# A two-layer Perceiver block on one core: a second cross attention queued by pairs of key tiles, three context buffers in the first, and GpSimd waits at three normalisations

## The reference

```python
x = x + _L0_xattn_ref(_layernorm(x, axis=-1), ctx_1024, L0_xattn_Wq, ...)       # one head of 128
x = x + _L0_attn_ref(_layernorm(x, axis=-1), ...)                               # 16 heads of 8
x = x + _L0_ffn_ref(_layernorm(x, axis=-1), L0_ffn_gate, ...)                   # experts, top 2
x = x + _L1_xattn_ref(_layernorm(x, axis=-1), ctx_1024, mask_Bx1x1xS2_ff0, ...) # 16 heads of 8
x = x + _L1_attn_ref(_layernorm(x, axis=-1), ...)                               # fake-quantised
x = x + _L1_ffn_ref(_layernorm(x, axis=-1), ...)                                # experts, top 2
```

```python
k = _split_heads(ctx @ kw + kb)
v = _split_heads(ctx @ vw + vb)
scores = jnp.einsum('bqhd,bkhd->bhqk', q, k) / np.sqrt(D // H).astype(np.float32)
scores = scores + mask
probs = jax.nn.softmax(scores, axis=-1)
out = jnp.einsum('bhqk,bkhd->bqhd', probs, v)
```

## Time and profile before

| | us |
|---|---|
| median of 3 runs | 1500.36 (1500.07 to 1515.0) |
| profiled execution | 1504.1 |
| its span | 1502.3 |
| start and first normalisation | 0 to 32.3 |
| first cross attention | 32.3 to 182.0 |
| a0 and the first experts | 182.0 to 528 |
| second cross attention, its first slots | 528 to 565 |
| its slots with scores and maxima | 565.0 to 1079.9 |
| the rest | to 1502.3 |

### The profile page before, as it was taken

The page is one execution under the profiler, slowest core; times in us unless marked ns, Lnnn a source line. Parts: engine busy times, 40 slices in busy tenths (PEclk is TensorE's granted clock), DMA queues, the critical chain, the costliest instruction groups (busy, mean ns, idle before and its releaser), DMA issues.

```text
span 1502.3 us, 24995 instructions
## 1 busy us (share of the span) xinstructions
PE 1132.7 (75%) x9454; PEld 829.9 (55%) x9454; DVE 784.9 (52%) x1546; ACT 495.5 (33%) x656; POOL 228.9 (15%) x234
## 2 busy tenths in 40 slices
PE   3766667588888358889989898898957644756987
PEld 2545444467777136666666666666644532545776
DVE  4223358543334355566666666556447547855111
ACT  0322223112222114544554454554513210321332
POOL 2000024202220200111111111111015101411110
PEclk9778869679999568999999999999979677766999
DMA  7444300101120133444434333343100000010111
GB/s 183 164 160 161 131 1 1 42 1 42 42 82 3 42 89 91 108 110 107 102 90 110 89 89 89 89 107 85 35 1 1 1 0 1 1 28 1 43 28 28
DMA packets 44859, 96.78 MB, mean 64 GB/s; under 512 B 12600, under 2 KB 28624, under 8 KB 44800
## 3 DMA queue, kind: packets, MB, share of 16 engines
q1 hardware_dynamic: 44800, 95.96, 24.2%
HBM read 41.04 MB, written 13.84 MB: 37 GB/s over the span
## 4 chain that ended last, share of the span: by engine, by line
PE 50%; issue 16%; DVE 14%; DMA 7%; POOL 5%; SPq 4%; ACT 3%; DVEq 0%; POOLq 0%; ACTq 0%
PE PS L261 46%; DMA KS<-kl 4%; DVE mx L1568 3%; PE PS L1192 2%; DVE u_all L274 2%; DVE kl L1557 2%; POOL work_area L389 2%; SPq L904 1%; DMA expert_area<-in_ctx 1%; DMA early<-in_ctx 1%; SPq L896 1%; POOL PT L389 1%; PE PS L1208 1%; PE PS L291 1%; POOL rstd_all L280 1%
## 5 line engine op out<-in xcount | busy, mean ns | idle before, releaser
L1568 DVE TENSOR_REDUCE mx<-PS 128x1 f32<-128x512 f32 (+1 forms) x512 | 278.3, 570 | 103.4 <-PE PS L261 96.0
L1135 ACT ACTIVATE PT<-PS 128x1024 f32<-128x1024 f32 (+1 forms) x208 | 212.3, 1021 | 62.6 <-PE PS L261 62.6
L261 PE MATMUL PS<-KS,QB 128*128 128x512 f32 (+1 forms) x512 | 178.9, 419 | 42.7 <-DVE mx L1568 22.1
L261 PE MATMUL PS<-QB,KS 128*128 128x256 f32 (+1 forms) x832 | 165.4, 321 | 18.6 <-DMA QB<-nml 18.6
L261 PE MATMUL PS<-QB,QS 128*128 128x512 f32 x576 | 158.0, 422 | 23.8 <-DVE wcol L662 21.7
L261 PEld LDWEIGHTS PS<-QB,KS 128*128 128x128 f32 (+1 forms) x832 | 115.7, 187 | 52.3 <-issue 28.1
L261 PEld LDWEIGHTS PS<-KS,QB 128*128 128x128 f32 x512 | 90.0, 191 | 94.9 <-issue 48.4
L261 PEld LDWEIGHTS PS<-QB,QS 128*128 128x128 f32 x576 | 108.7, 200 | 60.6 <-issue 26.8
L674 DVE SCALAR_TENSOR_TENSOR x<-PS,wcol,x 128x128 f32<-128x128 f32 x128 | 44.9, 351 | 137.0 <-PE PS L261 133.6
L291 PE MATMUL PS<-consts,u_all 128*128 128x128 f32 x64 | 15.7, 426 | 104.2 <-DVE u_all L274 83.6
L1121 ACT ACTIVATE kh<-PS,c_L_xattn_ck_b 128x512 fp32r<-128x512 f32 x64 | 38.1, 595 | 147.8 <-PE PS L261 123.7
(11 more groups left out here) (246 smaller groups left out, 1726.1 us busy)
## 6 DMA issues: line engine op xcount, KB each, us to landing
KS<-kh SPq DMA_DIRECT2D x128, 200.1 KB, 4.1
context_transposed<-ctxT SPq DMA_DIRECT2D x16, 800.5 KB, 3.5
ctxT<-context_transposed SPq DMA_DIRECT2D x16, 800.5 KB, 4.3
KS<-kl SPq DMA_DIRECT2D x64, 200.1 KB, 4.0
early<-in_ctx SPq DMA_DIRECT2D x8, 768.0 KB
expert_area<-in_ctx SPq DMA_DIRECT2D x8, 768.0 KB
expert_area<-in_L_ffn_experts_w SPq DMA_DIRECT2D x24, 256.0 KB, 3.2
expert_area<-in_L_ffn_W SPq DMA_DIRECT2D x16, 256.0 KB, 3.0
```

Of the source, the lines that this page charges most:

```text
L261: return T.matmul(o, l, r, start=start, stop=stop, **k)
L1135: P["exp_a"].done(S.activation(PT[0:rows, par, :], PS[0:rows, 1024 + 1024 * par:2048 + 1024 * par], ACT.Exp), f"e{k}")
L1568: P["max_v"].done(V.reduce_max(mx[:, p, c:c + 1], bank((4 * p + c) % 2, CHUNKS[c][1]), AX), item)
```

## The change

There are four parts.

1. First cross attention: a third context buffer in the free end of `work_area`. Pair n uses buffer n % 3; the load of pair 2 is issued behind the weights at the start, and later ones one pair earlier than before. The loops are written out, and TensorE takes the queries straight from `l0qk_all`, which moves to `u_all`.
2. GpSimd waits, at three of the nine normalisations, until VectorE has done its eight instructions.
3. In the attentions the row group alternates from matmul to matmul, instead of the bank or the block.
4. Second cross attention: tiles are grouped by two (`GROUPS`), with a second place for probabilities (`PT_TILES`), and the values of both tiles stand in one block of 16 matmuls. `steps(n)` reads one table for all engines. Key projections stand amid the maxima of a group, v2 and v3 at the end of the slot, and VectorE takes `sum` and each `kl` at the very place that they have in the table. SyncE issues the load of context n+2 between the first and the second key stack of slot n.

The diff, cut to its core:

```diff
-        ctx_nat = [a[:, :].rearrange("p (b k d) -> p b k d", b=2, k=KT) for a in (early, expert_area)]
         work_area = sb("work_area", [128, 3584 + KT * 256])
         tail_area, value_area = work_area[:, 0:3584], work_area[:, 3584:3584 + KT * 256]
+        ctx_nat = [a.rearrange("p (b k d) -> p b k d", b=2, k=KT)
+                   for a in (early[:, :], expert_area[:, :], tail_area[:, 0:2 * KT * 128])]
...
+        PT_TILES = [PT[:, :, :], tail_area[:, 0:2048].rearrange("p (a n) -> p a n", a=2)]
...
+        l0q, l0qk_all = prT[:, :], u_all[:, :, :].rearrange("p t d -> p (t d)")
...
-                for g in range(2):
-                    for c in range(2):
+                for c in range(2):
+                    for g in range(2):
...
-                    for g in range(2):
-                        for b in range(8):
+                    for b in range(8):
+                        for g in range(2):
...
-            pair(0, 0)
-            with eng.Fori(0, 3) as i:
-                pair(2 * i + 1, 1)
-                pair(2 * i + 2, 0)
-            pair(7, 1)
+            for n in range(PAIRS):
...
+        def steps(n):
+            tile = count = 0
+            for g, group in enumerate(SCHEDULE):
+                for step in group:
+                    if step == "s":
+                        if present("s", n):
+                            yield "s", g, tile
+                        tile += 1
+                    elif step == "pv":
+                        if g and present("s", n):
+                            yield "pv", g - 1, n
+                        elif not g and not (isinstance(n, int) and n < 1):
+                            yield "pv", len(GROUPS) - 1, n - 1
+                    elif step == "m":
+                        if present("m", n):
+                            yield "m%d%d" % MAXIMA[count], g, n
+                        count += 1
+                    elif present(step, n):
+                        yield step, g, n
...
+        def probs(group, q, tile, rows):
+
+            return PT_TILES[(group + q) % 2][0:rows, GROUPS[group].index(tile), :]
+
+        def load_pair(n):
+
+            q = n % 3
...
-                if c and n <= 0:
-                    at(nc.sync, "keys_v", "kl3", n + 1)
-                else:
-
+                at(nc.sync, "keys_v", "kl3", n + 1)
+                if not (c and n <= 0):
                     at(nc.sync, "exp_p", f"s{KT - 1}", n - 1)
                 nc.sync.dma_start(stack[98:100, :, :].bitcast(F32),
                                   mask_parts[:, bass.ds(n + 1, 1), :].broadcast_to([2, 4, KPAD])).then_inc(mask_stacked, 16)
...
                     for k, src in enumerate((kh, kh, kl)):
                         nc.sync.dma_start(stack[32 * k:32 * k + 32, g, 0:KEYS].bitcast(F32),
                                           src[32 * g:32 * g + 32, 0:KEYS].bitcast(F32)).then_inc(ks_stacked[g], 16)
-                if not (c and n > 12):
-
-                    at(nc.sync, "vals_p", "v3", n + 1)
-                    load_context(n + 3, 1 - q)
+                    if g == 0 and not (c and (n < 0 or n > 13)):
+
+                        at(nc.sync, "vals_p", "v3", n)
+                        load_context(n + 2, q)
...
             load_pair(1)
...
+            load_pair(2)
...
-            def save_and_load(n, q):
+            save(0)
+            for n in range(PAIRS - 1):
                 save(n + 1)
-
-                at(sp, "ca_p", "pc", n)
-                load_pair(n + 2, q)
-
-            save(0)
-            with sp.Fori(0, 3) as i:
-                save_and_load(2 * i, 0)
-                save_and_load(2 * i + 1, 1)
-            save(7)
+                if n < PAIRS - 3:
+                    at(sp, "ca_p", "pc", n)
+                    load_pair(n + 3)
...
             ln_all_gpsimd(0)
+            g.wait_ge(ln_xn, PAIRS)
...
             ln_all_gpsimd(2)
+            g.wait_ge(ln_xn, 3 * PAIRS)
             with g.Fori(0, EXPERTS // 2) as i:
                 moe_gpsimd("e0", True, i)
...
             ln_all_gpsimd(8)
+            g.wait_ge(ln_xn, 9 * PAIRS)
...
+            def values(n, g, q):
+                at(T, "exp_a", f"e{GROUPS[g][-1]}", n)
+                if g == 0:
...
+                for item, g, m in steps(n):
+                    if item == "s":
+                        scores(n, m, q)
+                    elif item == "pv":
+                        values(m, g, q if g < len(GROUPS) - 1 else 1 - q)
+                    else:
                         beside(item, n, q)
...
-                if not (isinstance(n, int) and n > 6):
-                    copy_queries(n + 1, 1 - q)
...
-                for k in range(KT):
-                    passed = side(n, k - 1) if k else []
-                    for item in passed + maxima(n, k) if k == 2 else maxima(n, k, 0) + passed + maxima(n, k, 1):
+                for item, g, m in steps(n):
+                    if item not in ("s", "pv") and item[0] != "v":
...
-SCHEDULE = ((1, "sum", 0), (2, "v0", 3), (3, "v1", 4), (4, "v2", 4), (5, "v3", 4), (6, "k0", 4),
-            (7, "k1", 4), (8, "k2", 4), (9, "k3", 5), (10, "nm", 0))
-
-PER = {"ca": 8, "a0": 6, "e0": 12, "a1": 4, "a2": 8, "e1": 12}
+GROUPS = ((0, 1), (2, 3), (4, 5), (6, 7), (8, 9), (10, 11), (12,))
+SCHEDULE = (
+    ("s", "s", "pv", "v0", "m", "m", "sum", "m", "m"),
...
+    ("s", "m", "s", "m", "pv", "m", "m", "k0", "m", "m"),
...
+IN_BANK7 = tuple(step for group in SCHEDULE for step in group if step not in ("s", "m", "pv"))
```

More of the change, by code:

```diff
@@ L819, in slots @@
                 slot(n, n % 2)
-        BESIDE = {k: ([], None) for k in range(KT)}
-        for k, side, count in SCHEDULE:
-            first = sum(len(b[0]) for b in BESIDE.values())
-            maxima = ["m%d%d" % MAXIMA[m] for m in range(first, first + count)]
-            BESIDE[k] = (maxima, side)
-        IN_BANK7 = ["sum", "v0", "v1", "v2", "v3", "k0", "k1", "k2", "k3", "nm"]
         def present(item, n):
-            c = isinstance(n, int)
+            if not isinstance(n, int):
+                return True
@@ L848, in bank7_free @@
         def bank7_free(item, n):
             before = [b for b in IN_BANK7[:IN_BANK7.index(item)] if present(b, n)]
[L851 to L860 removed]
+            m = n
@@ L861, in bank7_free @@
+            if not before:
+                m = n - 1
+                before = [b for b in IN_BANK7 if present(b, m)]
+                if isinstance(n, int) and n < -1:
+                    return
+            last = before[-1]
             if last == "sum":
@@ new lines, in scores @@
+            def scores(n, k, q):
+                rows = 128 if k < FULL else TAIL
+                par = (k + q) % 2
+                if k == 0:
+                    pe.wait_ge(nm_stacked, 32 * (n + 1))
+                if k >= 2:
+                    at(T, "exp_a", f"e{k - 2}", n)
+                elif not (isinstance(n, int) and n < 1):
+                    at(T, "exp_a", f"e{k + KT - 2}", n - 1)
+                for g in range(4):
+                    o = 1024 + 1024 * par + 256 * g
+                    last = mm(PS[0:rows, o:o + 256], KS[q][:, g, 128 * k:128 * k + rows], QB[q][:, 256 * g:256 * g + 256])
+                P["exp_p"].done(last, f"s{k}")
```

131 lines of the change are left out of this document (42 added, 89 removed), and 5 rows, old and new, of the table SCHEDULE.

## The result

The changed kernel takes 1537.92 us (median of 4 runs, 1532.37 to 1540.34), the kernel before 1500.95: ratio 1.0219, interval 1.0153 to 1.0285, 37 us slower. The forecast was 1522 us, slower by 21.8, with a range of 1488 to 1548.

The account below looks back on a forecast made before the run. It took late context loads to bound the first cross attention, and the TensorE-VectorE hand-over of two PSUM banks the second. Sum -32.2 - 10.5 + 0 + 64.5 = +21.8 us on 1500.4: 1522 us, range 1488 to 1548.

Parts of the forecast that it names:

- group 0: Second cross attention slot: two maxima ahead of VectorE's reciprocal, all others behind it; 4.3 us for 4 maxima.
- group 1: Second cross attention slot: the group free of both the reciprocal and the waits at kl; 4.75 us.
- the three key steps: Second cross attention slot: maxima around a key projection, VectorE's kl waiting for ScalarE's kh; 6.08 us for 6 maxima, three times.
- the last four: Second cross attention slot: the last four maxima, 1.8 us.
- +64.5 us: Second cross attention: each slot 4.3 us longer (+4.9 among the maxima, -0.6 to the next slot), times 15.
- rival 4: Second cross attention: stalls bring half clock, a quarter of each slot at 1.2 GHz, 15 x 2 us more: 1552 us; chance 0.10.
- the context's load among the stacks: SyncE in each slot: neither context nor second key stack comes late; cost 0, up to 1 us if the queue is slower.
- -32.2 us: First cross attention: a third buffer ends the waits for late context loads, gaining 5.37 us in each of six periods.
- the two stretches of pair 7 and pair 6: First cross attention: scores to exponential 6.82 us (pair 7), exponential to next scores 8.26 (pair 6); period 15.08 us.
- -10.5: GpSimd's waits at three normalisations give back VectorE's lost time: 3, 5.2 and 2.3 us; bounds 4 and 17.
- the row of the scores being nearest: Attentions' matmul order: value matmuls, between 0 and half of their time, taken as 0 after the row timing the scores.
- rival 3: Attentions: column halves run side by side for scores and values, 47 us, half on the path: 1499 us, no change; chance 0.05.

Follow-up runs that it names:

- kl_later: Changed kernel, but VectorE takes each kl behind the two maxima that follow its key projection, not ahead of them: 1505.9 us.
- the pass of sum: Changed kernel with kl behind two more maxima, the context load behind all four key stacks, and the row sums' reciprocal behind the third and fourth maximum: 1482.1 us.
- old_slot_two_buffers: Changed kernel with the second cross attention's slots as before and part 1 undone (two context buffers, loop, copied queries): 1479.7 us.

## Why the prediction was right in its sign and short in its size

**The slot.** The layout of the queues was right at full clock. Forecast 38.6 us, measured 37.99 to 38.84 in the five slots at clock 1.00, 38.4 in the mean. Cut as the forecast was, from first maximum to first maximum, these five give: group 0 4.1 us (forecast 4.3), group 1 4.9 to 5.9 (4.75), the three key steps 5.8 to 5.9, 5.7 to 5.8 and 5.7 (6.08 each), the last four 1.9 (1.8), together 28.2 to 29.2 (29.05). Group 1 was not free of everything, as I had it: in three of the five slots it waits for the second key stack. VectorE is idle in front of kl for 0.53 to 0.87 us, as forecast. TensorE does wait for VectorE four times a slot, but not for over 1 us each time: 0.77 to 1.36 us in front of the fifth maximum, behind the reciprocal, then, in most slots, 1.2, 1.15 and 0.16. That VectorE's order carries the loss was shown by kl_later and by the pass of sum.

The term of the sum that was mis-sized is +64.5 us: it is 74. The mean slot is 39.2 us, and the part above 38.4, 12 us in fifteen slots, goes with the clock. This is the mechanism of rival 4, to which I gave 0.10 as a case of its own. Ten of the fifteen slots had a mean granted clock of 0.85 to 0.96; nine of them took 38.35 to 41.23 us (the tenth projects no keys). In all ten but the first the half clock came right behind TensorE's wait for the first key stack, 1.4 to 3.0 us there, 0.93 before; but the five slots at 1.00 have waits of 1.3 to 2.1 us for it, so the length of this one wait doesn't decide it. It is an addition to the forecast, not an alternative. What it would take to keep the clock up there wasn't tried.

**The queue of SyncE.** I costed the context's load among the stacks at 0. It made them land 6.6 to 7.6 us after their issue, 4.0 before, and yet moving it gave back only 3 to 4 us. 0 was nearly right, and mostly by the reason stated (the second stack is needed late): TensorE waited for the second stack in five slots of fifteen, 4.3 us in all.

**Part 1.** Booked -32.2 us; undoing it costs 16 by the medians, 11 by the ratios, 22 in the traced stage. Two errors. The period was 16.05 us, not 15.08: pairs at full clock take 15.15, those at 0.90 take 16.56, and I had put the two stretches of pair 7 and pair 6 together as if the clock would hold. And the load of pair 2 ahead of the first save put that off not by 2.8 but by 5.4 us (37.15 to 42.55). ScalarE waited 13.33 us for it, so that the scores of pair 1 came 5.5 us later than in old_slot_two_buffers. I had named the wait, and sized it by the issue of a small transfer; the third and fourth issue took 1.84 and 1.48 us each.

**Part 2.** Booked -10.5; -5.6 by the medians, not clear of the noise. The second place is as computed, 4.9 us for the 5.2 booked. The first gave nothing, since the save, not the normalisation, then set the first exponential: the 3 us booked there had no path to the end. The 2.3 us of the third are not shown.

**Part 3.** Booked 0; it gains 10.6 us. The step that failed: "the row of the scores being nearest". The score matmuls have 512 columns, and the order changes nothing for them: four take 1.94 us at full clock in either. The value matmuls have 18 columns and overlap more in the new order. The Trainium skill ("TensorEngine Tiling (Array Packing)", "Key Properties") says that different tiles work in parallel. The value matmuls agree with it (1.06 us for 1.78); for the score matmuls no run here shows a gain. So rival 3 was half right.

Sum by the runs: +74 - 16 - 5.6 - 10.6 = +42, measured +37; the three were undone one by one, and each median carries 2 or 3 us. That the total came within 16 us is in part luck: the errors in the slots and in parts 1 and 2 add up to some 30 us, and the gain of part 3, booked at 0, took 10.6 of them back.

## What to carry to other kernels

When two engines hand two banks to and fro, an instruction that waits for a third engine must not stand directly ahead of their hand-over; put it two hand-overs later, and check each engine's queue by itself: one table for all engines puts kl on VectorE at the place of its projection on TensorE, before ScalarE has written kh. When a transfer is issued earlier, look at what stands behind it in its queue, with the issue time of a transfer of its own size; and when one is issued later, look at who then waits for it once the rest is faster. And price a stall of TensorE with what the clock may do behind it: here 38.4 us a slot became 39.2.

## What the runs showed of the hardware

Alternating the two halves of the output rows made matmuls of 18 columns overlap more (32 records in 1.06 us, 1.78 before) and did nothing for those of 512 columns (8 records in 1.94 us, before and after). A transfer of 0.8 MB issued between transfers of 0.2 MB took these from 4.0 to 6.6 and 7.6 us from issue to landing, and 4.0 to 4.1 when it was issued behind them. Of the four issues of one context load on SyncE the first two took 0.43 and 0.40 us, the third and fourth 1.84 and 1.48. Eight VectorE normalisations took 2.14 us with GpSimd held back, 8.71 and 9.40 beside its work.
